# Attention scores, two banks at a time: interleaving the products of a bank pair so that a stationary operand serves two consecutive products

## The reference, cut to what matters

```
x = X + attention(layernorm(X))
x = x + ffn(layernorm(x))

attention(X):
    Q = xpos(X @ W_Q);  K = xpos(X @ W_K, downscale=True);  V = X @ W_V
    scores = einsum('bqd,bkd->bqk', Q, K)            # 8 x 2048 x 2048
    p = softmax(scores, -1) * 0.9 ** |q - k|
    return einsum('bqk,bkv->bqv', p, V)

ffn(x):   h = silu(q4(x) @ q4(w_gate).T) * (q4(x) @ q4(w_up).T);  return q4(h) @ q4(w_down).T
```

## Time and profile before

| what | value |
|---|---|
| median of 3 runs | 2549.44 us (2548.57 to 2554.00) |
| span of the profiled execution, first to last instruction | 2546.6 us |
| TensorE matmul busy | 2518.4 us, 99% of the span, 16160 instructions |
| TensorE weight loads busy | 2290.0 us, 90%, 16160 instructions |
| VectorE, ScalarE, GpSimd busy | 84%, 59%, 71% |
| mean granted TensorE clock | 0.999 of full speed |

### The profile page before, as it was taken

How to read it: one execution, slowest core, us unless ns; L and a number is a source line. 1 busy time by engine, 2 the same in 40 slices (tenths; PEclk the granted TensorE clock), 3 DMA queues, 4 the chain that set the end, 5 groups by cost and what they waited for, 6 DMA issues and landing times.

```text
span 2546.6 us, 51904 instructions
## 1 busy us (share of the span) xinstructions
PE 2518.4 (99%) x16160; PEld 2290.0 (90%) x16160; DVE 2140.9 (84%) x4759; ACT 1489.8 (59%) x2966; POOL 1816.8 (71%) x1929
## 2 busy tenths in 40 slices
PE   8999999999999999999999999999999999999997
PEld 7888879999999999999999999999999999999996
DVE  8999878888878888888888888888888888888886
ACT  5766565656555655566565656565556655555654
POOL 6999956667767676667766776677666776677665
PEclk9999999999999999999999999999999999999999
DMA  8878511122111311131112111131113111211110
GB/s 285 302 271 299 186 50 30 34 86 66 38 40 45 107 37 42 34 106 42 42 34 91 62 38 40 45 107 39 42 34 106 41 42 34 95 58 38 40 38 22
DMA packets 163473, 203.27 MB, mean 80 GB/s; under 512 B 15184, under 2 KB 116752, under 8 KB 163216
## 3 DMA queue, kind: packets, MB, share of 16 engines
q1 hardware_dynamic: 163216, 200.01, 24.1%
HBM read 103.42 MB, written 77.59 MB: 71 GB/s over the span
## 4 chain that ended last, share of the span: by engine, by line
PE 85%; POOL 0%; DVE 0%; issue 0%; ACT 0%; POOLq 0%
PE score L516 27%; PE acc L655 19%; PE ring L516 19%; PE acc L516 9%; PE ring L622 6%; PE ring L675 3%; PE acc L697 1%; PE ring L613 1%; DVE hT L1226 0%; POOL probs L998 0%; ACT probs L823 0%; ACT hT L793 0%; POOL h_buf L1019 0%; POOL xv L1004 0%; POOL h_buf L1013 0%
## 5 line engine op out<-in xcount | busy, mean ns | idle before, releaser
L516 PE MATMUL score<-keys,q_st 128*128 128x512 f32 x3072 | 733.7, 394 | 3.0 <-ACT probs L823 2.6
L516 PEld LDWEIGHTS score<-keys,q_st 128*128 128x128 f32 x3072 | 567.0, 188 | 117.8 <-issue 3.0
L998 POOL TENSOR_TENSOR probs<-probs,decay 128x512 f32<-128x512 f32 (+3 forms) x416 | 450.7, 1097 | 197.5 <-ACT probs L823 197.5
L655 PE MATMUL acc<-vals,pT 128*128 128x256 f32 x3984 | 554.6, 286 | 0.8 <-DVE pT L1226 0.8
L516 PE MATMUL ring<-w_gu,xqT 128*128 128x512 f32 (+1 forms) x2304 | 509.1, 374 | 0.0
L655 PEld LDWEIGHTS acc<-vals,pT 128*128 128x128 f32 x3984 | 498.1, 189 | 7.3 <-DVE pT L1226 2.0
L516 PEld LDWEIGHTS ring<-w_gu,xqT 128*128 128x128 f32 x2304 | 419.0, 188 | 63.6 <-DVE xqT L1226 0.4
L793 ACT ACTIVATE xqT<-ring 128x256 fp32r<-128x256 f32 x128 | 49.3, 385 | 706.9 <-PE ring L613 706.9
L1239 DVE TENSOR_REDUCE smax<-score 128x1 f32<-128x1024 f32 x256 | 312.8, 1222 | 95.6 <-PE score L516 94.1
L1226 DVE TENSOR_TENSOR pT<-ring,pT 128x512 fp32r<-128x512 f32 (+3 forms) x432 | 248.7, 600 | 66.7 <-ACT pT L793 65.5
L1004 POOL TENSOR_TENSOR xv<-xv,xe 128x256 f32<-128x256 f32 x128 | 94.4, 737 | 269.1 <-DVE xv L1079 269.1
(11 more groups left out here) (133 smaller groups left out, 4470.0 us busy)
## 6 DMA issues: line engine op xcount, KB each, us to landing
k_dram<-keys SPq DMA_DIRECT2D x56, 512.0 KB, 4.5
keys<-k_dram SPq DMA_DIRECT2D x56, 512.0 KB, 7.3
edge<-vals SPq DMA_DIRECT2D x288, 64.0 KB, 2.1
q_raw<-q_dram SPq DMA_DIRECT2D x129, 128.0 KB, 2.6
x_in<-X SPq DMA_DIRECT2D x32, 512.0 KB, 4.5
q_dram<-q_stage SPq DMA_DIRECT2D x32, 512.0 KB, 5.4
x_res<-X SPq DMA_DIRECT2D x128, 128.0 KB, 2.1
out<-x_res SPq DMA_DIRECT2D x128, 128.0 KB, 1.7
```

The source lines that it names most:

```text
L516: mm = pe.matmul(dst, stat(a, k), mov(m, k), start=i == 0, stop=ends and i == n - 1)
L655: mm = pe.matmul(pv_out, pT[g % 2][:, a, j * P:(j + 1) * P], edge[places[m]][:] if kb in edges else vals[m][:, kb, :], start=i == 0, stop= ...
L998: op = pool.tensor_tensor(probs[:, k0:k1], probs[:, k0:k1], decay[:, off + k0:off + k1], ALU.mult)
```

## The change

The loop over four banks becomes a loop over two pairs of banks. Inside a pair the order of the loops is turned over: for each half `k` and pass `(a, m)` there are two products with the same stationary operand, one into each bank of the pair, and the groups of accumulation of both banks are open at once. The waits of the two banks stand together ahead of the pair. The number of products, the operands of each, the order of summation in each bank and the place where `scored` is raised stay as they are.

```diff
-                for o in range(4):
-                    if s == 0 and at[2] is not first_plan:
-                        pe.wait_ge(k_back[o], at[0] * 32)
+                for h in range(2):
+                    pair = range(2 * h, 2 * h + 2)
+                    for o in pair:
+                        if s == 0 and at[2] is not first_plan:
+                            pe.wait_ge(k_back[o], at[0] * 32)
+                        if s == 0 and at[2] is first_plan:
+                            pe.wait_ge(k_split, (B - 1) * NC + o + 1 + PRIME)
                     if s == 0 and at[2] is first_plan:
-                        pe.wait_ge(k_split, (B - 1) * NC + o + 1 + PRIME)
-                        if o % 2 == 0:
-                            pe.wait_ge(rotated, 2 * NCH - 1 + o // 2 + PRIME)
+                        pe.wait_ge(rotated, 2 * NCH - 1 + h + PRIME)
                     elif s == 1 and at[2] is first_plan:
-                        if o % 2 == 0:
-                            pe.wait_ge(exped, 2 * g - 1 + o // 2)
-                    elif o == 0:
+                        pe.wait_ge(exped, 2 * g - 1 + h)
+                    elif h == 0:
                         pe.wait_ge(exped, 2 * g)
-                    mm = product(score[:, o, :], lambda a, k: q_st[s % 2][:, a, k, :],
-                                 lambda m, k: keys[m][:, k, o * CH:(o + 1) * CH], range(KT))
-                    if o % 2:
-                        mm.then_inc(scored, 1)
-                    if o == 1 and begun_between:
+                    for i, (k, (a, m)) in enumerate((k, p) for k in range(KT) for p in PASSES):
+                        for o in pair:
+                            mm = pe.matmul(score[:, o, :], q_st[s % 2][:, a, k, :], keys[m][:, k, o * CH:(o + 1) * CH],
+                                           start=i == 0, stop=i == KT * len(PASSES) - 1)
+                    mm.then_inc(scored, 1)
+                    if h == 0 and begun_between:
                         attend_begun(at, s - 1)
```

## The result

The changed kernel takes 2554.53 us (median of 15 runs, 2552.86 to 2556.05), the kernel before 2549.77 us (15 runs, 2548.31 to 2554.02). The ratio is 1.0017, 95% interval 1.0010 to 1.0024 (the ratio on record isn't the quotient of the two medians, which is 1.0019): 4.8 us slower. That is inside the 0.2%, 5.1 us, that the prediction counts as the same, but the interval leaves out 1 and reaches above 1.0020. The profiled execution of the changed kernel has a span of 2553.1 us, against 2546.6.

The account below looks back on a forecast made before the run. The prediction took TensorE's stream of products as the bound, 2518.4 of 2546.6 us. Product order 0, batch starts 2.7 and the very first step 0.8 us made 3.5 us, from 2549.4 to 2553.0 us, range 2547.5 to 2560.

Parts of the forecast that it names:

- Term 1: Score products on TensorE: the new order leaves their spacing at 0.227 us, so it costs and gives 0 us.
- Rival 4: Score products on TensorE: the repeated stationary operand pays, 14 us less from 1024 products, 2539 us; chance 0.08.
- rival 5: Score products on TensorE: alternating banks costs 9 ns for each product of a second half, 14 us, 2567 us; chance 0.07.
- Term 2: Seven batch starts in the loop: product 13 waits for bank 3's keys at six, 1.9 + 0.8 = 2.7 us.
- The last transfer lands, issue plus duration: Batch starts: last key landings, 577.5 to 2232.1, set against product 13's starts; six waits, 1.86 us together.
- Term 3: Very first step: product 13 waits for the split keys, scores end 1.36 us later, the next step 0.8 us late.
- The sum: Whole kernel: 0 + 2.7 + 0.8 = 3.5 us more, median from 2549.4 to 2553.0 us.
- Rival 2: Batch starts: keys land in time, only the very first step's 0.8 us is left, 2550.2 us; chance 0.15.
- rival 3: Batch starts: keys land 0.7 us later than profiled, mean wait about 1 us, 8.7 us in all, 2558 us; chance 0.10.
- The forecast: Whole kernel: the prediction's own case, 2553 us, its own range 2551 to 2555; chance 0.60.
- Four things hang on the order: Score steps: `scored`, the `exped` wait and the transposes stay, costing nothing; only key waits of banks 1 and 3 move.

Follow-up runs that it names:

- four-bank order: Against the kernel before: in inner steps one stationary operand serves four consecutive products, one into each bank; first step of each batch keeps the old order; 2722.31 us, ratio 1.0681.
- reverse experiment: Against the kernel before: old order of products, only the waits for keys of banks 1 and 3 moved ahead of products 1 and 13; 2555.26 us, ratio 1.0022.

## Why the prediction was right

**Term 1, the order of the products: 0 us, and 0 measured.** It was read from three transitions in one step, and four runs bear it out: the new order alone is at ratio 1.0003, no repeats at 0.9999, 23 repeats of 24 at 1.0001, each with an interval that holds 1, and all of them, like the four-bank order, still take 5.72 us for 24 products. Rival 4 (14 us less) and rival 5 (14 us more) are both out. The Trainium skill says in "TensorE: Matmul & The Clock Gate", "Step-by-step: what each phase is for", that a separate load lets one load once and multiply repeatedly. No run here shows that: each of these kernels has 3072 loads for 3072 products, repeated operand or not, so repeating the operand is worth nothing, and what products without a load would be worth wasn't tried. Why the 512 columns take 0.227 us and not 213 ns stays open; it isn't which operand is loaded. One bound was misread on the way. The 9 ns a product by which the first half of a step is dearer, from which rival 5 has its 14 us, are not spread over twelve products: in the trace of the kernel before product 2 starts 0.314 us behind product 1, which is most of it.

**Term 2, the batch starts: forecast 2.7 us, 4.6 us in the profile.** Mechanism and place are as forecast, and the reverse experiment, waits alone, gives the whole price. That there are six stops, as forecast, is in part luck, since they aren't the same six. The size is off for two reasons, both in the step "The last transfer lands, issue plus duration". The first: I let product 13 start at the landing, and it starts later. The last key transfer of the first start in the changed kernel's trace is this:

```profile
L433 SPq DMA_DIRECT2D keys<-k_dram x1: 778/778/778, 569.2 to 569.2; - x1
...
DMA to landing us min/median/max: 10.1/10.1/10.1
```

It landed at 569.2 + 10.1 = 579.3 us and product 13 started at 579.41, 0.1 us behind it. In the unrounded times of the trace it is 0.135 us at each of the six stops, 0.8 us together. The second: the landings moved. Here the transfer took 10.1 us, where the same one took 9.2 us before, and was issued 0.3 us closer to product 1; so this start, forecast with 0.7 us to spare, stopped, while the one at 1404.54, forecast to wait 0.52 us, had 0.50 us to spare. From landing to the place of product 13 the six waits are 0.50, 0.44, 0.07, 0.94, 0.18 and 1.00 us, 3.1 us together against the 1.86 of the forecast. That accounts for the rest, some 1.2 us. The scatter of single landings was the weak point of a sum of tenths; the range had it, the central value leaned on one execution. The restart, forecast at 0.13 us, is 0.1 us (3.00 us for twelve products against 5.72 - 2.84 = 2.88 us).

**Term 3, the very first step: forecast 0.8 us, 0.87 us in the profile,** by the chain as written: twelve products behind a stop of 1.77 us (forecast 1.8), and the second maximum late.

**The sum: forecast 3.5 us, measured 4.8 us,** 2553.0 against 2554.53 us, so the price was 1.4 times the forecast one; the miss is the size of term 2. Rival 2 (keys in time) is out, rival 3 was nearer than its chance said: it asked for a mean wait over 0.5 us, and the profiled execution had (4.6 - 0.7) / 7 = 0.56 us with the 0.7 us of restarts taken off, so by its own mark it lies just on the side of rival 3. The forecast and rival 3 are one mechanism, and the measured time lies between their centres on the side of the forecast. "Four things hang on the order" in the prediction held as well, and the four-bank run shows what the first of them was worth: that `scored` is raised at product 12 is the part of the old order that the kernel can't spare.

## What to carry to other kernels

When a loop over outputs is turned inside out to reuse an operand, look first for whether the reuse saves anything: two products in the old trace, one with a repeated operand and one without, gave the answer before any run. Then list what was tied to the old order: each wait that moves ahead costs its landing minus the new place, and each completion that moves back delays what is queued behind its reader on that engine, which may belong to another tile. If the interleaving is wanted for other reasons, put each wait at the product that reads the data; that brought the price from 4.8 us to 0.5 us, which is no longer clear of the noise.

## What the runs showed of the hardware that wasn't expected

- With all waits at product 1, each stop of TensorE at the start of a batch, 2.1 to 4.6 us long, was followed by 7 to 14 products about 0.43 us apart, at the lower clock; the stops of up to 1.8 us in the changed kernel were not. That an idle TensorE falls back to half rate is also what the Trainium skill says in "TensorE: Matmul & The Clock Gate", Part 1, and the trace agrees: clock 0.51 in the stretch behind a stop of 3.33 us. The length of the stop alone doesn't decide it. The second step of the first batch waits 2.25 us in the kernel before and has its twelve products in 2.99 us, at clock 1.00; the kernel without repeats waits as long in the same place and takes 4.58 us, at clock 0.50:

```profile
321.69 4.58 PE L516 MATMUL score<-keys,q_st 128*128 128x512 f32 x12 [2.24 <-ACT probs L823]
```

  Why it fell in one and not in the other stays open.
- In the drain at the end, where TensorE waits for other engines between short bursts, the lower clock comes and goes from execution to execution. In the stretch from 2510 to 2520 us the kernel before had 1.00 and the changed one 0.83:

```profile
2510.00:2520.00 10.00, 7.77 (x44) 7.12 (x43) 6.58 (x16) 2.72 (x7) 5.98 (x6) 0.83 0.09 26
```

  The two profiled spans differ by 6.5 us, 5.5 us of it from the two places above. The attention starts 0.3 us earlier in the changed kernel, and from the last product of the scores to the end it takes 1.3 us longer. Nothing suggests that this belongs to the change: the mean granted clock is 0.9983 over the 15 runs of the changed kernel and 0.9984 over 31 runs of the kernel before.
- The first products of the scores behind the transposes are further apart than 0.227 us: 0.314 us from product 1 to 2, then 0.224 to 0.236 us up to the eleventh. In the inner step at about 1795 us they are the same within 1 ns, position by position, in the kernel before, the changed one, the one without repeats and the one with a single operand, and product 13 starts 2.84 us after product 1, whatever the order of the banks and the repeats. What causes it wasn't tried.
